# Where the product with the token numbers is made in the token table's rounds: VectorE or GpSimd

## The reference, cut to what matters

```python
probs = jax.nn.softmax(xf @ router_w.T, axis=-1)
topv, topi = jax.lax.top_k(probs, 2)
topv = topv / (topv.sum(axis=-1, keepdims=True) + 1e-09)
cw = (jax.nn.one_hot(topi, e, dtype=xf.dtype) * topv[..., None]).sum(axis=1)
h = jax.nn.gelu(jnp.einsum('td,edh->teh', xf, w1), approximate=False)
y = jnp.einsum('teh,ehd->ted', h, w2)
out = jnp.einsum('te,ted->td', cw, y)
```

## Time and profile before

| | us |
|---|---|
| median of three runs | 1058.36 |
| lowest and highest | 1057.31, 1061.56 |
| the profiled execution | 1060.01 |
| its span, first to last instruction | 1058.0 |
| TensorE busy | 910.3 |
| VectorE busy | 621.1 |
| ScalarE busy | 512.5 |
| GpSimd busy | 423.3 |

### The profile page before, as it was taken

The page is one execution under the profiler, slowest core; times in us unless marked ns, Lnnn a source line. Parts: engine busy times, 40 slices in busy tenths (PEclk is TensorE's granted clock), DMA queues, the critical chain, the costliest instruction groups (busy, mean ns, idle before and its releaser), DMA issues. The chain is left out here.

```text
span 1058.0 us, 23850 instructions
## 1 busy us (share of the span) xinstructions
PE 910.3 (86%) x7874; PEld 627.0 (59%) x7874; DVE 621.1 (59%) x1484; ACT 512.5 (48%) x865; POOL 423.3 (40%) x592
## 2 busy tenths in 40 slices
PE   5799999997027999999999999995479888879996
PEld 3445656554016889898988989874124444445552
DVE  4567888876795444454444444322768888645561
ACT  1478888875311333323333333342266666645663
POOL 2377777762102423333221222212865665104451
PEclk9789999999557999999999999998568999999999
DMA  6323444334420111112111121112324222000212
GB/s 181 72 77 99 137 125 133 111 102 148 163 79 20 54 49 45 57 41 61 41 49 53 42 61 41 51 46 70 100 70 112 67 71 56 1 1 5 54 45 61
DMA packets 73727, 75.42 MB, mean 71 GB/s; under 512 B 22730, under 2 KB 66874, under 8 KB 73626
## 3 DMA queue, kind: packets, MB, share of 16 engines
q1 hardware_dynamic: 67146, 56.31, 17.9%
q0 software_dynamic: 6480, 17.70, 6.5%
HBM read 51.64 MB, written 22.34 MB: 70 GB/s over the span
## 5 line engine op out<-in xcount | busy, mean ns | idle before, releaser
L1496 DVE CAST hh_e<-h_e 128x512 f16<-128x512 f32 x128 | 59.4, 464 | 178.1 <-ACT h_e L1446 105.3
L1347 PE MATMUL up_ps<-xT_e,experts 128*128 128x256 f16 x512 | 139.6, 273 | 0.7 <-DVE xT_e L1488 0.6
L1361 PE MATMUL y_ps<-experts,hh_e 128*128 x512 | 139.6, 273 | 0.0
L1362 PE MATMUL y_ps<-experts,hh_e 128*128 x512 | 139.6, 273 | 0.0
L1348 PE MATMUL up_ps<-xT_e,experts 128*128 128x256 f16 x512 | 139.6, 273 | 0.0
L1363 PE MATMUL y_ps<-experts,hh_e 128*128 x512 | 139.6, 273 | 0.0
L1349 PE MATMUL up_ps<-xT_e,experts 128*128 128x256 f16 x512 | 139.6, 273 | 0.0
L1273 POOL COPY idx_e<-token 128x2 int32 (+2 forms) x39 | 22.5, 577 | 286.4 <-PE xT_ps_e L1322 237.0
L1446 ACT ACTIVATE h_e<-up_ps 128x512 f32<-128x512 f32 x128 | 76.4, 597 | 87.5 <-PE up_ps L1349 87.5
L1498 DVE TENSOR_TENSOR hh_e<-h_e,hh_e 128x512 f16<-128x512 f32 x128 | 88.6, 692 | 4.4
L1763 ACT ACTIVATE prob_a<-sT_ps_a 77x1024 f32<-77x1024 f32 x64 | 64.9, 1015 | 42.1 <-PE sT_ps_a L1667 42.1
(11 more groups left out here) (328 smaller groups left out, 2115.0 us busy)
## 6 DMA issues: line engine op xcount, KB each, us to landing
experts<-in_L_ffn_w SPq DMA_DIRECT2D x22, 512.0 KB, 4.1
y_scratch<-y_e SPq DMA_DIRECT2D x32, 256.0 KB, 3.4
x<-in_x SPq DMA_DIRECT2D x32, 128.0 KB, 3.3
experts<-in_x SPq DMA_DIRECT2D x64, 64.0 KB, 2.5
x_scratch<-x SPq DMA_DIRECT2D x16, 256.0 KB, 2.5
xh_scratch<-xn SPq DMA_DIRECT2D x16, 256.0 KB, 2.8
w_r<-in_L_ffn_w SPq DMA_DIRECT2D x8, 512.0 KB, 4.3
x_a<-x_scratch SPq DMA_DIRECT2D x32, 128.0 KB, 2.6
```

The lines of the kernel that those rows point to most:

```text
L1347: mm(out, w[0], xT[0][:, c, 0:W_], start=c == 0, stop=False)
L1361: mm(out, a[0], w[0], start=m == 0, stop=False)
L1362: mm(out, a[0], w[1], start=False, stop=False)
```

## The change

GpSimd gets a list of instructions in `route`: it waits until the three constant tables are there, and in each round for both comparisons, and then does the product. VectorE has neither the product nor the wait in front of it.

```diff
+            @block.gpsimd
+            def _(pool):
+                pool.wait_ge(s_ids, 3)
+                for q in range(NT // Q):
+                    pool.wait_ge(s_hot, 2 * q + 2)
+                    nc.gpsimd.tensor_tensor(tokhot[:, q % 2, :, :], halfhot[:, q % 2, :, :],
+                                            tokenid[:, None, flat(q, 2 * Q)].broadcast_to([P, HALFT, 2 * Q]), ALU.mult) \
+                        .then_inc(s_tile, 1)
+
             @block.vector
...
                     v.tensor_tensor(rowhot[:, q % 2, :, :], rowid[:, :, :],
                                     part(lo_f, q)[:, None, :].broadcast_to([P, P, 2 * Q]), ALU.is_equal).then_inc(s_hot, 1)
-                    dve.wait_ge(s_hot, 2 * q + 2)
-                    v.tensor_tensor(tokhot[:, q % 2, :, :], halfhot[:, q % 2, :, :],
-                                    tokenid[:, None, flat(q, 2 * Q)].broadcast_to([P, HALFT, 2 * Q]), ALU.mult).then_inc(s_tile, 1)
                     if q + 2 < CHUNKS:
                         weights(q + 2)
```

## The result

The changed kernel took 1062.51 us (median of 16 runs, 1060.02 to 1065.43) against 1058.72 for the kernel before (16 runs, 1054.92 to 1061.85): ratio 1.0035, interval [1.0021, 1.0048]. The forecast was +4.1. Two executions of one experiment's kernel, at a lower granted clock over their whole length (1553 us at 0.55, where the others have 0.92 to 0.93), stand in no ratio here.

A forecast was written before the change was run, and what follows sets the result against it. The routing, short only of VectorE, delays TensorE's expert work. Rowhot 7 ends 3.58 later, the tail saves 0.48 and adds 0.97: L1226 moves +4.07, so 1058.4 + 4.1 = 1062.4 us, range 1056.0 to 1066.8.

The forecast's parts named there:

- The exclusion: In the rounds, GpSimd's reading product and VectorE's two-input instructions exclude each other; without it 3.4 us less, with it slower.
- Rival 1: In the rounds, the port isn't shared by f16 instructions and the product hides: -3.4, 1055.0; chance 0.06.
- rival 2: In the rounds, only the conversions hold GpSimd: -2.4 to -1.4, about 1056.5; chance 0.08.
- Who comes first: After rowhot the weights conversion goes first, 1.14; the product then gets in before the next halfhot, 1.01.
- the turn at the end of an instruction: When the weights conversion ends, the waiting GpSimd product gets in between, ahead of VectorE's next halfhot, held 0.32 more.
- Rival 3: VectorE keeps the port; the product runs only when VectorE stands at s_tab: +5.8, 1064.2; chance 0.12.
- The product's size: Each of eight GpSimd products takes 1.15 us for 568 elements; ends 1.12 and 1.61.
- rival 4: The GpSimd product is dear, 1.61, 0.46 more in each of eight rounds: +7.8, 1066.1; chance 0.12.
- The sum: Rounds with a conversion take 3.07 against 2.60; rowhot 7 ends +3.58, L1226 starts at 329.1 against 325.04, +4.07.
- the tail: Behind the rounds, VectorE's product is saved, 0.48 less, but one two-input instruction is held by product 7, +0.97.
- Covers: TensorE's last round, done about 327.4, stays hidden; ScalarE's weights copies, ready at 310.7 and 313.5, stand before VectorE in time.
- The clock: Behind the token table, a clock rise up to 2 us late adds 1 us, as likely some gained; taken as nothing.

The follow-up runs named there:

- one experiment's kernel: Kernel before, with ScalarE making the product in rounds 0 and 2, VectorE behind the conversion in the others; ratios 0.9986 and 0.9979 on two occasions.
- The zeros: Changed kernel, with GpSimd writing zeros into tokhot instead of the product, reading no tensor; ratio to the kernel before 0.9968.
- the doubled product: Changed kernel, with GpSimd making each product twice, the second after the first has ended; ratio to the kernel before 1.0075.
- a copy: Changed kernel, with GpSimd only copying halfhot to tokhot instead of multiplying; ratio to the kernel before 1.0006.
- a reduction: Changed kernel, with VectorE reducing a loaded weights chunk in the conversion's place in rounds 0 to 5, the six conversions behind the table; 1067.17 us.

## Why the prediction was right

- *The exclusion, and so the sign.* Read in the earlier trace rows from other places and with f32 among the operands, it held for f16 comparisons too. Rival 1 (1055.0) and rival 2 (1056.5) fall by halfhot at 1.38. The zeros show nearly what rival 1 would have looked like: 18.0 for the stretch, 3.9 less than before; rival 1 has 3.4 less, because a product of 1.15 would let round 7 wait 0.5 for TensorE.
- *Who comes first, and the turn at the end of an instruction.* One place in the earlier trace rows with a tiny operation bore it; the rounds with a conversion, the doubled product and the row at 62.41 confirm it. Rival 3 falls.
- *The product's size.* 1.13 against 1.15 taken from the line through the earlier trace rows; rival 4 (1.61) falls. The row length of eight elements costs nothing that shows. The Trainium skill (GPSIMD Engine Reference, Elementwise — side-by-side cycle accounting) measures about 2.6 cycles an element for an f32 sum; at 1.2 GHz that is an estimate of 1.23 for 568 elements, before any start-up. The 1.13 measured here, in f16, lies below, and decides.
- *The sum.* From rowhot's end in round 0 to that of round 5 15.19 against 15.35 (five rounds of 3.04, not 3.07); to round 6 3.04 against 3.07; to round 7 2.13 against 2.16, with a wait for TensorE of 0.45, where the prediction has 0.40; the tail 4.31 against 4.33, with the first two-input instruction in it (L1222) held to 1.12. Together 3.83 against 4.07; the 0.24 is 0.03 in each of seven rounds and 0.02 in the tail. In a round, 0.02 of it is the product (0.99 behind the conversion, not 1.01) and some 0.01 halfhot's rest (0.31, not 0.32).
- *Covers.* ScalarE's last two high halves were ready at 312.3 and 315.5, and their conversions came at 318.4 and 321.45. TensorE was done at 329.2, 1.8 before L1232. Both as predicted.
- *The clock* was taken as nothing. By the granted clock (0.69 on average over 334 to 339 us, 1.00 behind) it rose from 1.2 to 2.4 GHz near 337.1, that is 5.4 us behind GpSimd's index copy; before, near 332.5, it was 6.7. The work behind the table so gained some 0.6 us of the profiled span.
- *Signs.* Halfhot at 1.38, one instruction of the tail longer by 0.95, and L1232 at 331.00, which less the late start of 2.13 is 328.9 against 329: as written. The products are recorded at 2.05 and not 2.2, because that sum counted the 0.14 twice.

The median moved by 3.8, the stretch by 3.83. That these two agree so closely is luck: the interval of the times leaves 2.2 to 5.1, and the profiled spans differ by 4.7. What bears out the forecast is the trace. The Trainium skill (SBUF — State Buffer, Who interferes with whom) states both halves of the rule: two inputs of SBUF on VectorE, and reading on GpSimd. The runs agree with each: held by 0.93 with a product, by 0.45 with a copy, by nothing with zeros, by 0.02 behind a reduction.

## What to carry to other kernels

Before moving work from VectorE to GpSimd, look at what VectorE runs meanwhile. If it is instructions with two tensors of SBUF, or casts like L1496, and GpSimd's work reads SBUF, that work isn't parallel but another entry in VectorE's queue, at GpSimd's price: here VectorE stood 0.93 a round for the 0.49 that it was spared. The trace of the kernel before tells it at no cost: look for a short GpSimd operation that is long somewhere, and for what VectorE ran then. And when the gain sought is a wait between dependent instructions, put other work of the same engine into it first; that kept its 0.12 a round.

## What was not expected of the hardware

- An activation of ScalarE over 71 elements, every eighth of a row, with a scale read from a tile for each partition: eight of them took 2.82, some 0.31 from start to start, each recorded at 0.62. The one of 64 elements in `route` is recorded at 0.24, from which 0.2 had been guessed. Which of stride and scale costs it was not tried.
- Whoever had waited got the port when the other's instruction ended, even where the other had its next one ready: VectorE yielded so in all six rounds of the doubled product that have a conversion, GpSimd in three places of the kernel before.
- A cast of VectorE with one input, 0.42 as a rule, was held to 1.27 by a reading GpSimd instruction; a reduction of 1.21 with one input did not hold GpSimd's product (1.13).
